# Attention output of a decoder layer turned and divided in 32x32 blocks on VectorE instead of by TensorE's turns, with the query rotation on GpSimd

## The reference, cut to what matters

```python
x = _layernorm(x + _L0_attn_ref(x, ...))            # linear attention, 32 heads of 8
x = _layernorm(x + _L0_xattn_ref(x, ctx, ...))      # softmax attention over ctx, 16 heads of 16
x = _layernorm(x + _L0_ffn_ref(x, ...))             # low-rank FFN: 256 -> 64 -> 1024 (gelu) -> 64 -> 256
```

```python
q = _rope2d((query @ Wq.T).reshape(B, Nq, H, D).transpose(0, 2, 1, 3).astype(float16), qpos)
k = _rope2d((key @ Wk.T)....astype(float16), kpos)
attn = softmax(einsum('bhqd,bhkd->bhqk', q, k) * scale, axis=-1)
x = einsum('bhqk,bhkd->bhqd', attn, v).transpose(0, 2, 1, 3).reshape(B, Nq, C)
return x @ Wo.T + bo
```

## Time and profile before

| | |
|---|---|
| median of 3 runs | 586.6 us (586.26 to 589.58) |
| the profiled execution: its own time, its span | 589.89 us, 588.1 us |
| TensorE matmul busy | 536.4 us (91% of the span) |
| VectorE busy | 405.6 us (69%) |
| ScalarE busy | 344.7 us (59%) |
| GpSimd busy | 278.7 us (47%) |
| mean granted TensorE clock | 0.969 of 2.4 GHz |

### The profile page before, as it was taken

How to read it: one execution, slowest core, us unless ns; L and a number is a source line. 1 busy time by engine, 2 the same in 40 slices (tenths; PEclk the granted TensorE clock), 3 DMA queues, 4 the chain that set the end, 5 groups by cost and what they waited for, 6 DMA issues and landing times.

```text
span 588.1 us, 11834 instructions
## 1 busy us (share of the span) xinstructions
PE 536.4 (91%) x4236; PEld 367.9 (63%) x4236; DVE 405.6 (69%) x912; ACT 344.7 (59%) x505; POOL 278.7 (47%) x317
## 2 busy tenths in 40 slices
PE   6996989999999999999999999999797678999993
PEld 3884767676767676767767676767464345555551
DVE  6578786969687878788787869696967521344444
ACT  3452556566666666666757575666565566565651
POOL 6566344464655554637374655545441122242424
PEclk9998899999999999999999999999997889999997
DMA  8653111204020302021113202120101010032322
GB/s 268 142 111 74 37 31 57 69 1 103 4 85 7 98 9 78 29 77 30 57 33 73 77 10 57 49 69 1 32 4 31 18 55 19 26 119 93 121 89 107
DMA packets 29130, 35.99 MB, mean 61 GB/s; under 512 B 5720, under 2 KB 15320, under 8 KB 29080
## 3 DMA queue, kind: packets, MB, share of 16 engines
q1 hardware_dynamic: 28216, 34.37, 20.2%
q10 hardware_dynamic: 864, 0.95, 0.5%
...
...
## 4 chain that ended last, share of the span: by engine, by line
PE 60%; DVE 16%; issue 13%; POOL 5%; ACT 4%; DMA 1%; POOLq 1%; SPq 0%; ACTq 0%
PE FR L1158 20%; PE BK L1158 8%; PE BK L1326 8%; DVE nmax L989 7%; PE SC L1283 5%; PE SC L1311 4%; PE FR L1243 3%; PE FR L1371 2%; PE FR L1221 2%; DVE lin_tm L900 2%; POOL rs L604 2%; POOL c_fm L609 2%; PE BK L1343 2%; PE SC L1158 2%; DVE y L1025 2%
## 5 line engine op out<-in xcount | busy, mean ns | idle before, releaser
L989 DVE TENSOR_REDUCE nmax<-SC 128x4 f32<-128x1024 f32 x128 | 156.1, 1220 | 31.8 <-PE SC L1283 30.9
L718 ACT ACTIVATE probs<-SC 128x1024 f32<-128x1024 f32 x128 | 130.9, 1023 | 70.1 <-PE SC L1311 69.9
L1326 PE MATMUL BK<-probs,v_aug 128*32 128x256 f32 x1024 | 70.5, 393 | 0.6 <-ACT probs L718 0.6
L1283 PE MATMUL SC<-k_blk,q_grp 48*128 48x512 f16 x256 | 51.4, 399 | 18.3 <-DVE nmax L989 18.3
L522 POOL TENSOR_TENSOR rs<-ve,minus_half 128x2 f32<-128x2 f32 x16 | 11.2, 700 | 95.3 <-DVE nm L1031 95.3
L499 POOL TENSOR_TENSOR att_fm_l<-att_raw,att_fm_h 128x512 fp32r<-128x512 f32 x16 | 20.5, 1283 | 74.6 <-ACT att_raw L693 74.6
L1311 PE MATMUL SC<-q_grp,k_blk 64*128 64x256 f16 x512 | 50.5, 275 | 3.4 <-ACT q_grp L675 1.8
L811 ACT ACTIVATE probs<-SC,b_ff 128x512 f32<-128x512 f32 x64 | 39.8, 686 | 22.5 <-PE SC L1532 21.7
L1326 PEld LDWEIGHTS BK<-probs,v_aug 128*32 128x32 f32 x1024 | 27.0, 111 | 26.4 <-issue 14.9
L1283 PEld LDWEIGHTS SC<-k_blk,q_grp 48*128 48x128 f16 x256 | 12.4, 93 | 46.0 <-DVE nmax L989 24.6
L1311 PEld LDWEIGHTS SC<-q_grp,k_blk 64*128 64x128 f16 x512 | 25.0, 97 | 21.5 <-ACT probs L718 4.3
...
## 6 DMA issues: line engine op xcount, KB each, us to landing
...
k_blk<-k_rope SPq DMA_DIRECT2D x128, 16.0 KB, 1.8
...
```

Source lines behind the costliest of these rows:

```text
L718: act.activation(probs[:, j % 4], SB[:], ACT.Exp, scale=SCALE).then_inc(s_exp, 1)
L989: dve.tensor_reduce(nmax[:, t, :, 2 * q:2 * q + 2], src[:].rearrange("p (s f) t -> p s f t", s=2), AX.X, ALU.max, negate=True).then_inc(s_ ...
L1283: mm = pe.matmul(out[:, 2 * s:2 * s + 2].rearrange("p h t -> p (h t)"), q_grp[n % NB][rows, q, t * P:(t + 1) * P], k_blk[n % NB][rows, q]. ...
L1326: mm = pe.matmul(BK[q // 2][HP * k:HP * (k + 1), (q % 2) * T:(q % 2 + 1) * T], v_aug[b % NB][:, t, HC * q + k], probs[:, j % 4, k], start= ...
```

## The change

`ev_pv`, `o_t` and `att_t` are gone. VectorE's block transpose, which turns each 32x32 square by itself and leaves the squares where they are, now reads the PSUM banks directly (`turn_pv`): since four heads lie at 32 partitions each, a square holds one head and 32 tokens, and after the turn the tokens of one square lie on partitions and the head's 16 outputs and its sum lie side by side. `att_norm` takes one reciprocal and two products from there, and turns the result back with a third block transpose, straight into `att_raw`. The order of features that results is met by another order of the rows of `w_o2`. `ev_att` keeps one copy (att_raw to att_fm_h, now from SBUF). `wo(LAST)` and its neighbours stand in another order behind the last step.

Of the queries' rotation VectorE keeps `q_halves` (the shuffle); the two products and the sum are GpSimd's `rope_q` for n of 2 and more. GpSimd's step has another order: `rope_k` ahead of `att_lo`, `residual_bias` ahead of `keep_x2`, `rope_q` behind it.

```diff
@@ GpSimd
+            def rope_q(n):
+                cos, sin = (t[:, n * T:(n + 1) * T].unsqueeze(1).broadcast_to([P, CC, T]) for t in (cos_t, sin_t))
+                pool.wait_ge(s_q2_ev, n + 1)
+                pool.tensor_tensor(q_cos[:], q16[:], cos, ALU.mult).then_inc(s_q_part, 1)
+                pool.wait_ge(s_q_rot, n + 1)
+                pool.tensor_tensor(q_sin[:], rot[:], sin, ALU.mult).then_inc(s_q_part, 1)
+                wait(pool, s_s2_mm, NQ * (n - 2))
+                pool.wait_ge(s_q_part, 2 * n + 2)
+                pool.tensor_tensor(q_grp[n % NB][:].rearrange("p (c e) t -> p e c t", e=2)[:, 0], q_cos[:], q_sin[:],
+                                   ALU.add).then_inc(s_q_rope, 1)
@@ GpSimd, step
+                if on(n):
+                    rope_k(n)
                 if on(p):
                     att_lo(p)
-                if on(n):
-                    rope_k(n)
+                if on(m):
+                    residual_bias(m)
                 if on(q):
                     keep_x2(q)
                 if on(n):
+                    rope_q(n)
+                if on(n):
                     residual2(n)
@@ ScalarE
-            def ev_pv(b, half):
...
             def ev_att(p):
-                act.wait_ge(s_att_mm, p + 1)
-                act.activation(flat(att_fm[0][:]), BK[1][:], ACT.Copy).then_inc(s_att_hi, 1)
-                act.activation(flat(att_raw[:]), BK[1][:], ACT.Copy).then_inc(s_att_raw, 1)
+                act.wait_ge(s_att_raw, p + 1)
+                wait(act, s_wo_mm, p)
+                act.activation(flat(att_fm[0][:]), flat(att_raw[:]), ACT.Copy).then_inc(s_att_hi, 1)
@@ VectorE
+            def turn_pv(b, half):
+                dve.wait_ge(s_pv_mm, NQ * b + NQ // 2 * (half + 1))
+                dve.transpose(o_tok[:, 2 * half:2 * half + 2].rearrange("p q b r -> p (q b r)"), BK[half][:]
+                              ).then_inc((s_pvc_ev, s_pvd_ev)[half], 1)
+
             def att_norm(p):
...
+                dve.wait_ge(s_pvc_ev, p + 1)
+                dve.wait_ge(s_pvd_ev, p + 1)
+                dve.reciprocal(rden2[:], o_tok[:, :, :, D2]).then_inc(s_rden2, 1)
+                dve.wait_ge(s_rden2, p + 1)
+                out = flat(lin_tm[:]).rearrange("p (q b u d) -> p q b u d", q=2, b=T // HP, u=2)
+                for half in range(2):
+                    part = slice(2 * half, 2 * half + 2)
+                    dve.tensor_tensor(out[:, :, :, half], o_tok[:, part, :, 0:D2],
+                                      rden2[:, part].unsqueeze(3).broadcast_to([P, 2, T // HP, D2]), ALU.mult
+                                      ).then_inc(s_att_ev, 1)
+                dve.wait_ge(s_att_ev, 2 * p + 2)
+                wait(dve, s_attt_ev, p)
+                dve.transpose(flat(att_raw[:]), flat(lin_tm[:])).then_inc(s_att_raw, 1)
@@ behind the last step: VectorE
+            turn_pv(LAST, 1)
+            att_norm(LAST)
             stats2(LAST - 1)
-            att_norm(LAST)
             add2(LAST)
@@ behind the last step: TensorE (att_t gone)
             h_ff(0, 5)
+            wo(LAST)
+            u2_ff(0, 2)
             x2_t(LAST - 1)
-            wo(LAST)
             p_ff(LAST - 1)
-            u2_ff(0, 2)
```

More of the change, by code:

```diff
@@ L805, in _ @@
             exp_chunk(LAST, 7)
-            ev_pv(LAST, 1)
             act.sem_inc(s_gelu, 4)
@@ L823, in _ @@
             ev_att(LAST)
-            gelu(0, 2)
-            gelu(0, 3)
+            for f in range(2, 6):
+                gelu(0, f)
             ev_x2t(LAST - 1)
-            gelu(0, 4)
+            gelu(0, 6)
             ev_p(LAST - 1)
-            for f in range(5, NF):
-                gelu(0, f)
+            gelu(0, 7)
             ev_x2t(LAST)
@@ L1048, in step @@
                     stats1(n)
+                if on(p):
+                    turn_pv(p, 1)
                 if on(n1):
@@ L1066, in step @@
                 if on(n):
-                    rope_q(n)
+                    q_halves(n)
                 if on(q):
                     ev_p(q)
+                if on(p):
+                    add2(p)
                 if on(n1):
                     row_max(n1, 5)
-                if on(p):
-                    add2(p)
+                if on(b):
+                    turn_pv(b, 0)
                 if on(m):
@@ L1329, in pv @@
                 mm.then_inc(s_pv_mm, 1)
-            def o_t(p, t):
-                if t == 1:
-                    pe.wait_ge(s_pvc_ev, p + 1)
-                    pe.wait_ge(s_pvd_ev, p + 1)
-                elif on(p + 4):
-                    pe.wait_ge(s_kv1_ev, 2 * (p + 4) + 1)
-                elif p + 4 == B:
-                    pe.wait_ge(s_proj_ev, B)
-                else:
-                    pe.wait_ge(s_p_ev, p - 1)
-                for q in range(H2 // HC):
-                    mm = pe.transpose((FR[1], BK[1])[t][:, q * P:(q + 1) * P], o_fm[:, q, t * P:(t + 1) * P], ident[:])
-                mm.then_inc(s_ot_mm, 1)
-            def att_t(p):
-                pe.wait_ge(s_att_ev, 2 * p + 2)
-                turn(BK[1], lin_tm, s_att_mm)
             def wo(p):
@@ L1362, in x2_t @@
                     pe.wait_ge(s_vk_ev, q + 6)
-                if q == LAST:
-                    pe.wait_ge(s_p_ev, LAST)
+                elif q + 5 == B:
+                    pe.wait_ge(s_proj_ev, B)
+                else:
+                    pe.wait_ge(s_p_ev, q)
                 turn(FR[1], x2_tm, s_x2t_mm)
@@ L1520, in _ @@
             pv(LAST, 7)
-            o_t(LAST, 1)
-            o_t(LAST, 0)
             pe.sem_inc(s_u2_mm, 4)
@@ L1570, in _ @@
             h_ff(0, 1)
-            att_t(LAST)
             h_ff(0, 2)
@@ L1608 @@
     by_group = [D2 * h + d for h in HEADS for d in range(D2)]
+    by_turned = [D2 * HEADS[HC * (2 * half + q) + k] + d
+                 for q in range(2) for k in range(HC) for half in range(2) for d in range(D2)]
     inv_freq = np.float32(1.0) / np.float32(100.0) ** (np.arange(0, 8, 2, dtype=np.float32) / np.float32(8))
```

47 lines of the change are left out of this document (11 added, 36 removed).

## The result

Median 603.91 us (602.31 to 604.06, 4 runs) against 587.70 us (586.26 to 589.58, 4 runs) of the kernel before on the same chip: ratio 1.0275, 95% interval 1.0242 to 1.0308. The change makes the kernel slower by 16 us. The profiled execution took 604.06 us with a span of 602.2, 14.1 more than the span before.

What follows compares the result with a forecast made beforehand. VectorE was taken to hold the path in each step's second half, TensorE in the first. 0.65 + 0.44 = 1.09 a step, 12.0 us over 11, ends about -0.1, gave a median of 598.4 us; range 588 to 612.

Steps and rivals of the forecast that it cites:

- What TensorE sheds: First half of a step: o_t and att_t go, 1.29 us, paid back as waiting for wo.
- The price of a turn: One VectorE block transpose of 512 words was put at 0.65 us, bounds 0.45 and 1.23.
- dear turns: Rival: a VectorE turn costs 1.23 us, +2.24 a step, 611 us; chance 0.10.
- Second half +0.65: From p_ff's end to the next first score product: one turn lies wholly on VectorE's path to scores1(7), +0.65 us.
- First half +0.44: From first score product to p_ff's end: wo starts at 268.74 instead of 268.30, behind att_lo, +0.44 us.
- (a): VectorE: the upper bank's turn fills the 0.66 us idle ahead of the third row maximum, costing nothing.
- (c): GpSimd: att_lo, now behind the keys' rotation, ends at 268.69, so wo starts 0.44 us later.
- (b): VectorE: GpSimd's SBUF read holds back the first attention product; the row maximum after the turn comes 0.68 us later.
- The ends -0.1: Steps outside the 11 full ones and the way behind the last: together about -0.1 us, 3 us either way.
- No blocking: Rival: VectorE's attention products run beside GpSimd unhindered, step +0.47, 592 us; chance 0.13.
- Faster: Rival: turns fall into VectorE's idle time, att_lo comes before TensorE, about 1.0 us gained a step, 575 us; chance 0.15.
- The clock: Rival: TensorE's waits for vk_sb and wo lower its clock, wo and p_ff slow down, 608 us; chance 0.12.

Runs made afterwards that it cites:

- copy_lower: The changed kernel with the attention output's lower bank copied by ScalarE and turned by VectorE at the next step's start; 599.29 us, ratio 1.0213.
- split_late: The changed kernel with split_x(m+1) moved behind att_lo(p) on GpSimd; 596.29 us, ratio 1.0175.
- att_first: The changed kernel with att_lo(p) put back ahead of rope_k(n) on GpSimd; 589.86 us, ratio 1.0077.
- stats_first: The changed kernel with stats2(14) put back ahead of the last turn and att_norm(15) on VectorE, behind the last step; 597.72 us, ratio 1.0202.
- quiet_tail: The changed kernel with split_c behind the shift, att_lo ahead of k_sin, split_x behind k_rope, and stats2(14) and stats2(15) earlier behind the last step; 579.63 us, ratio 0.9895.

## Why the prediction was right, and where it was not

The median, 603.9, lies in the range and 5.5 us over the forecast of 598.4, at the edge of the forecast's own range (593 to 604). Of that, 2.2 are in the spans, +14.1 instead of the predicted +11.9. 1.1 is the median of before, 587.7 in this comparison instead of 586.6; and 2.2 come from scaling: the profiled execution before lay 2.2 over the median 587.7, that after is at its own.

- **What TensorE sheds** comes back as waiting. Right: TensorE 0.84 less busy in a step, and the step 0.98 longer.
- **The price of a turn**, 0.65 with bounds 0.45 and 1.23: 0.71 long, 0.63 to the next start, 0.60 by taking it away. Right; the rival of dear turns fell.
- **Second half +0.65**: measured +0.47. The turn costs what it should; the step that failed is "Swapping add2 and the maximum moves nothing in the sum". From p_fm to the row maximum ahead of scores1(7) VectorE needed 4.03 before and 4.51 after. Before, the maximum to the start of add2 took 1.26 (244.12 to 245.38); after, from 247.53 to the turn, 1.13. copy_lower shows the same 0.12 to 0.13 without the turn. The swap also moved the waiting: the one wait of 1.1 ahead of scores1(7) that was to show the forecast did not come; there are two of 0.47, ahead of scores1(6) and scores1(7).
- **First half +0.44**: measured +0.50. Counted from the first score product, the steps (a) to (c) held to 0.05 us: fourth row maximum 11.18 predicted, 11.17 measured; k_sin 12.85 and 12.80; att_lo 15.29 and 15.25; wo 16.62 and 16.58. The 0.06 too little is that p_ff comes 0.1 later behind a wo that waited. (b), the blocking, is shown by split_late (and by the first product's 1.13, its end 10.16 behind the first score product, as forecast), (c), the place of att_lo, by att_first.
- **The rotation costs GpSimd alone nothing.** They "end some 9.5 us after att_lo, ahead of the next norm; nobody waits for them" was right for this kernel, but by luck: in the kernel after, cs_fm_l ends 1.0 us ahead of `shift`. Put into the kernel before, the same three instructions cost 0.4 us a step. I had asked when they end and who waits, and not what VectorE does while they run.
- **Eleven full steps at 1.09, 12.0**: 10.0. Ten took +0.97 and step 12 only +0.3.
- **The ends -0.1**: +4.1, the largest miss. Step 0 -1.6 (-1.0), step 1 +0.2 (0), steps 13 and 14 together -1.0 (-2.1), each subject to the clock as said above, and from the last shift turn +6.7, for which I had -1.6 + 4.6 = +3.0. stats2(14)'s part, 4.6, has the right size, in part by luck: stats_first gave back 4.7, but 1.4 of it is the way from wo(15) to p_ff(14), 5.3 us in the kernel after and 4.0 in att_first, whose programs are the same there and whose clock was higher. wo(15) itself came 3.1 earlier. Two things failed. The -1.6 came out as -0.2 at p_ff(14) in stats_first: wo(15) was 2.5 earlier than before (25.7 behind the shift turn instead of 28.2), but u2_ff(0, 2) and x2_t(14) now stand between it and p_ff(14), 3.88 from wo to p_ff instead of 1.54. And I had no term for what lies behind p_ff(14), where the kernel after loses another 2.4: 1.3 up to p_ff(15), by gelu(0, 6) ahead of ev_p(14), and 1.0 after it, whose cause is open.

  Step 15 itself became only 0.6 shorter (the last pv ends 20.2 us behind the shift turn instead of 20.8), and the clock has a part in that. Windows from the last shift turn to the last pv, in the kernel before, in stats_first, and in quiet_tail, whose step 15 has the same programs as that of stats_first:

```profile
468.64:489.42 20.78, 14.86 (x148) 7.68 (x146) 5.44 (x19) 13.32 (x17) 7.35 (x9) 0.90 0.12 39
477.84:498.08 20.24, 15.04 (x137) 7.04 (x135) 7.36 (x21) 11.99 (x14) 7.12 (x9) 0.71 0.11 40
461.21:480.54 19.33, 14.01 (x137) 6.83 (x135) 7.36 (x21) 11.99 (x14) 7.12 (x9) 0.81 0.12 42
```

  The same work took 0.9 us less at a mean clock of 0.81 than at 0.71.

- **No blocking** fell (split_late). **Faster** fell: att_lo did not come before TensorE. Its 575 was nearly reached, 576 to 578, once att_lo's place, the two collisions and the lower turn were mended, but only half by its mechanism: a full step got 0.55 to 0.67 shorter and not 1.0, and the rest lies in the ends, which gained by a move that is no part of the change.
- **The clock**, as a rival, fell for the full steps: TensorE stood still four times in each, 0.55, 0.73 and twice 0.47, and the granted clock stayed 1.00 (the window above). Behind longer waits it did fall: in step 13 (2.04 for a row maximum, until 431.07, a wait that the kernel before has too) and behind the last step (3.04 and 2.18 for GpSimd). Windows of the kernel after:

```profile
436.00:440.00 4.00, 4.00 (x30) 1.99 (x28) 3.60 (x8) 2.47 (x4) 1.41 (x2) 0.53 0.00 0
505.00:510.00 5.00, 4.50 (x20) 3.21 (x20) 0.69 (x1) 0.47 (x1) 0.00 (x0) 0.70 0.03 11
515.00:520.00 5.00, 2.13 (x8) 1.59 (x8) 0.21 (x2) 0.60 (x1) 3.06 (x4) 0.82 0.11 43
```

In step 13 and behind the last step the mean fell to 0.53, 0.70 and 0.82 (the lower level, 1.2 GHz, is 0.50), and p_ff(15) took 2.07 us instead of 1.13. So a wait in the ends can cost more than its length. How much of the +2.3 of step 13 is the clock was not separated; the kernel before also shows a dip to 0.63 there (424 to 428).
